# Reordering the steps of a fused attention and int8 layer, with two PSUM banks for the first projections

## What is computed

```python
q = (x @ Wq + bq).reshape(b, t, H, D)
k = (x @ Wk + bk).reshape(b, t, HKV, D)
v = (x @ Wv + bv).reshape(b, t, HKV, D)
q = q * cos + rotate_half(q) * sin
k = k * cos + rotate_half(k) * sin
attn = jnp.einsum('bikgd,bjkd->bkgij', qg, k) * scale      # causal mask, softmax
out = jnp.einsum('bkgij,bjkd->bikgd', p, v).reshape(b, t, H * D)
x = _layernorm(x + out @ Wo)
q, in_scale = per_token_quant_int8(x)                        # round(x / scale), scale = absmax / 127
acc = jnp.einsum('bsk,nk->bsn', q, weight)
x = _layernorm(x + (acc * in_scale * w_scale + bias).astype(float16))
```

## Time and profile before

| what | value |
|---|---|
| median of three runs | 174.61 us (174.49 to 174.62) |
| the profiled execution, its own time | 174.22 us |
| its span, first to last instruction | 172.3 us |
| instructions in it | 4469 |
| share of the span busy: TensorE, VectorE, ScalarE, GpSimd | 85%, 82%, 71%, 50% |
| mean granted clock of TensorE | 0.957 |

### The profile page before, as it was taken

How to read it: one execution, slowest core, us unless ns; L and a number is a source line. 1 busy time by engine, 2 the same in 40 slices (tenths; PEclk the granted TensorE clock), 3 DMA queues, 4 the chain that set the end, 5 groups by cost and what they waited for, 6 DMA issues and landing times. The chain is left out here.

```text
span 172.3 us, 4469 instructions
## 1 busy us (share of the span) xinstructions
PE 147.3 (85%) x1552; PEld 87.3 (51%) x1552; DVE 140.8 (82%) x345; ACT 123.0 (71%) x231; POOL 85.7 (50%) x191
## 2 busy tenths in 40 slices
PE   1768999999999999999999989999999988893330
PEld 0154464565665556656676456655666554551100
DVE  3408789898899599899899789989999997787582
ACT  3244577887797879898988776989878898993000
POOL 1051794224078868213899996032488504465111
PEclk9999999999999999999999999999999999997555
DMA  5986000000000001000000101000001200001101
GB/s 138 259 142 186 2 5 0 4 4 0 10 4 0 6 0 65 1 6 1 2 8 0 56 12 59 8 0 8 0 2 47 80 4 2 2 4 61 61 0 61
DMA packets 5463, 5.63 MB, mean 33 GB/s; under 512 B 1217, under 2 KB 4674, under 8 KB 5442
## 3 DMA queue, kind: packets, MB, share of 16 engines
q1 hardware_dynamic: 5298, 5.16, 10.9%
q10 hardware_dynamic: 144, 0.20, 0.4%
HBM read 3.12 MB, written 2.10 MB: 30 GB/s over the span
## 5 line engine op out<-in xcount | busy, mean ns | idle before, releaser
L415 ACT ACTIVATE prob<-score_ps 128x512 bf16<-128x512 f32 x160 | 89.6, 600 | 16.8 <-PE score_ps L616 8.2
L507 DVE TENSOR_REDUCE nmax<-front_ps 128x1 f32<-128x320 f32 (+21 forms) x137 | 87.6, 680 | 13.2 <-PE front_ps L660 12.3
L612 PE MATMUL score_ps<-qkA 128*128 128x512 bf16 x160 | 57.9, 379 | 0.9 <-ACT prob L415 0.5
L658 PE MATMUL front_ps<-qkA 128*128 128x384 bf16 (+9 forms) x176 | 50.6, 334 | 1.7 <-DVE nmax L507 1.4
L627 PEld LDWEIGHTS mix_ps<-qkv,prob 128*128 128x128 bf16 x640 | 26.1, 96 | 14.3 <-ACT prob L415 3.5
L660 PE MATMUL front_ps<-tab 128*128 128x32 bf16 (+2 forms) x176 | 32.3, 187 | 0.0
L627 PE MATMUL mix_ps<-qkv,prob 128*128 128x17 bf16 x640 | 30.2, 171 | 1.3 <-ACT prob L415 1.2
L658 PEld LDWEIGHTS front_ps<-qkA 128*128 128x128 bf16 x176 | 17.2, 98 | 16.6 <-issue 6.8
L616 PE MATMUL score_ps<-tab 128*128 128x512 bf16 x64 | 24.2, 378 | 0.0
L424 ACT ACTIVATE qkA<-side_ps 128x1024 bf16<-128x1024 bf16 x16 | 16.4, 1024 | 5.5 <-PE side_ps L649 5.3
L354 POOL TENSOR_TENSOR rot<-qkv,tab 128x320 bf16<-128x320 bf16 x14 | 10.4, 745 | 18.6 <-ACT qkv L420 18.6
(11 more groups left out here) (61 smaller groups left out, 175.6 us busy)
## 6 DMA issues: line engine op xcount, KB each, us to landing
out<-fo SPq DMA_DIRECT2D x7, 256.0 KB, 2.2
xt<-in_xT SPq DMA_DIRECT2D x1, 768.0 KB, 6.3
qkA<-peakT SPq DMA_DIRECT2D x32, 4.0 KB
xt<-in_xT SPq DMA_DIRECT2D x2, 128.0 KB, 3.0
bfc<-in_bias SPq DMA_DIRECT2D x2, 128.0 KB, 7.4
out<-fo SPq DMA_DIRECT2D x2, 128.0 KB, 1.7
tab<-in_table SPq DMA_DIRECT2D x1, 232.0 KB, 3.1
wqkv<-in_wqkv_in ACTq DMA_DIRECT2D x1, 192.0 KB
```

The lines of the kernel that those rows point to most:

```text
L415: act.activation(prob[:, u % PROB_RING, :].rearrange("p (h t c) -> p t h c", h=GH, c=SUB), score_ps[u % SCORE_RING][:, :].rearrange("p (t ...
L507: dve.tensor_reduce(to, src, AX.X, ALU.max, negate=True).then_inc(max_ok, 1)
L612: mm = pe.matmul(score_ps[u % SCORE_RING][:, :].rearrange("p (t c) -> p t c", c=TOK), qkA[:, n, GH + g, TOK * j:TOK * (j + 1)], qkA[:, n, ...
L658: pe.matmul(bank, qkA[:, n, t, TOK * i:TOK * (i + 1)], qkA[:, n, GH + g:GH + g + fit, 0:wide], start=True, stop=False)
```

## The change

Three things. First, TensorE runs 26 matmuls of a one-row constant with itself into `mix_ps` before it waits for the weights. Nothing reads the result. Second, the projections P1, P2 and P3 (`HEAD_TILES`) write `dense_ps` instead of `side_ps`; their copies and ropes wait for that bank's semaphores. Third, all five lists of `ORDER` have another order, with the same steps in each. Other additions are switched off or have no user: `LINEAR_ACT` is False and `NORM_FAST` is 0, the steps n, d and l on ScalarE, r on VectorE and N on GpSimd stand in no list, and `rden` has two slots instead of one.

```diff
+LINEAR_ACT = False
+HEAD_TILES = (1, 2, 3, )
+WARM = 26
+NORM_FAST = 0
...
     "tensor": """
-        P0 P1 P2 T0 T1 F0 F1 F2 F3 F4 T2 F5 F6 G0 F7 F8 F9 P3 F10 F11 F12 P4 S0 S1 F13 F14 F15 P5 S2 F16 F17 T3 F18 S3 F19 F20
+        P0 P1 P2 T0 P3 F0 T1 F1 F2 F3 F4 F5 T2 F6 F7 F8 F9 P4 F10 F11 G0 F12 P5 F13 F14 F15 T3 F16 F17 S0 F18 G1 S1 F19 F20 W0
...
     "gpsimd": """
-        R2 w0 K0 R3 K1 R4 R5 K2 R6 R7 K3 K4 K5 m0 R8 Q0 R9 K6 R10 H0 z0 Y0 R11 K7 m1 K8 Q1 K9 m2 R12 Q2 R13 H1 H2 K10 z1 Y1 z2
-        R14 Y2 R15 m3 K11 K12 Q3 K13 m4 Q4 H3 K14 H4 z3 Y3 z4 Y4 m5 K15 Q5 m6 H5 z5 Y5 m7 z6 m8 z7 z8
+        R2 R3 K0 w0 R4 K1 R5 K2 R6 R7 K3 m0 R8 K4 Q0 R9 K5 H0 z0 K6 R10 Y0 R11 m1 K7 K8 Q1 R12 m2 K9 R13 H1 Q2 z1 K10 Y1 H2 z2
+        R14 m3 Y2 K11 R15 K12 Q3 m4 K13 Q4 H3 H4 z3 Y3 K14 z4 Y4 m5 K15 Q5 m6 H5 m7 z5 Y5 m8 z6 z7 z8
...
-SIDE_USES = [step for step in steps("tensor") if step[0] in "PTG"]
-DENSE_USES = [step for step in steps("tensor") if step[0] in "UMDL"]
+def in_dense(step):
+
+    return step[0] in "UMDL" or step[0] == "P" and step[1] in HEAD_TILES
+
+
+SIDE_USES = [step for step in steps("tensor") if step[0] in "PTG" and not in_dense(step)]
+DENSE_USES = [step for step in steps("tensor") if in_dense(step)]
...
+        def project_bank(u):
+
+            if u in HEAD_TILES:
+                return dense_ps, dense_full, dense_free, dense_at("P", u)
+            return side_ps, side_full, side_free, side_at("P", u)
...
                 elif kind == "p":
-                    act.wait_ge(side_full, side_at("P", u) + 1)
-                    act.activation(qkv[:, u, :, 0:VAT + DH], side_ps[:, 0:PC].rearrange("p (g c) -> p g c", g=GROUPS),
-                                   ACT.Copy).then_inc(side_free, 1)
+                    bank, filled, freed, uses = project_bank(u)
+                    act.wait_ge(filled, uses + 1)
+                    act.activation(qkv[:, u, :, 0:VAT + DH], bank[:, 0:PC].rearrange("p (g c) -> p g c", g=GROUPS),
+                                   ACT.Copy).then_inc(freed, 1)
...
             pe.wait_ge(ones_set, 1)
+            for _ in range(WARM):
+                pe.matmul(mix_ps[:, 0:128], ones[:, :], ones[:, :], start=True, stop=True)
             pe.wait_ge(weights_in, 16 * 2)
```

More of the change, by code:

```diff
@@ L121 @@
-        N13 X135 X136 B5 s6 q5 a6 B6 d5 q6 l5 N14 d6 l6 Z5 H6 s7 Z6 a7 B7 N15 Y6 q7 s8 a8 B8 d7 q8 l7 H7 d8 Z7 l8 H8 Y7 Z8 Y8
+        R0 R1 X0 X1 X2 X3 X4 X5 X6 X7 X8 X9 X10 X11 X12 X13 X14 X15 X16 X17 X18 X19 X20 N0 X21 X22 X23 X24 X25 X26 X27 X28 X29
+        N1 X30 X31 X32 X33 X34 s0 X35 X36 X37 X38 X39 B0 X40 X41 N2 X42 X43 q0 X44 X45 X46 d0 X47 X48 l0 X49 X50 X51 X52 X53
+        Z0 X54 X55 X56 X57 N3 X58 X59 X60 N4 X61 X62 X63 X64 s1 X65 X66 X67 X68 X69 N5 X70 X71 X72 X73 B1 X74 X75 s2 X76 X77
@@ L226, in build @@
         qsc = sb("qsc", [128, ALL], bf16)
+        qscf = sb("qscf", [128, ALL], fp32)
+        mixs = sb("mixs", [128, 2, HEADS * VA], fp32)
         qrec = sb("qrec", [128, ALL], fp32)
@@ L441, in _ @@
                         one.then_inc(dense_free if m == ms[-1] else x1_ok, 1)
+                elif kind == "n":
+                    act.wait_ge(weighed, LAST_SCORE[u] + 1)
+                    need(act, att_ok, u - 1)
+                    act.activation(mixs[:, u % 2, :], mix_ps[:, 0:HEADS * VA], ACT.Copy).then_inc(mixed_ok, 1)
+                elif kind == "d":
+                    ms, part, done = tiles_of(u)
+                    act.wait_ge(dense_full, dense_at("D", u) + 1)
+                    act.activation(q8T[:, KC * ms[0]:KC * done, :],
+                                   dense_half[:, 0:KC * TOK * len(ms)].rearrange("p (a c) -> p a c", c=TOK),
+                                   ACT.Copy).then_inc(dense_free, 1)
+                elif kind == "l":
+                    ms, part, done = tiles_of(u)
+                    act.wait_ge(dense_full, dense_at("L", u) + 1)
+                    for m in ms:
+                        one = act.activation(fo[:, m, :], dense_ps[:, (m - ms[0]) * HID:(m - ms[0] + 1) * HID], ACT.Copy,
+                                             scale=qscf[:, m:m + 1])
+                        one.then_inc(dense_free if m == ms[-1] else fo_ok, 1)
                 elif kind == "Y":
@@ L541, in _ @@
                     dve.wait_ge(qsc_ok, done)
+                    if LINEAR_ACT and u not in FAST:
+                        dve.tensor_copy(qscf[:, part], qsc[:, part])
                     dve.reciprocal(qrec[:, part], qsc[:, part]).then_inc(qrec_ok, len(ms))
@@ L623, in _ @@
                     if u == FIRST_SCORE[tile]:
-                        need(pe, att_ok, tile)
+                        if tile <= NORM_FAST:
+                            need(pe, mixed_ok, tile)
+                        else:
+                            need(pe, att_ok, tile)
                     pr = prob[:, u % PROB_RING, :].rearrange("p (h c) -> p h c", h=GH)
@@ L632, in _ @@
                         pe.wait_ge(xt_in[(0, 2, TILES).index(u)], 16)
-                    pe.matmul(side_ps[:, 0:PC], ones[:, :], bqkv[:, :], start=True, stop=False)
+                    bank, filled, _, _ = project_bank(u)
+                    pe.matmul(bank[:, 0:PC], ones[:, :], bqkv[:, :], start=True, stop=False)
                     for c in range(KC):
-                        mm = pe.matmul(side_ps[:, 0:PC], xt[:, c, TOK * u:TOK * (u + 1)], wqkv[:, c, :],
+                        mm = pe.matmul(bank[:, 0:PC], xt[:, c, TOK * u:TOK * (u + 1)], wqkv[:, c, :],
                                        start=False, stop=c == KC - 1)
-                    mm.then_inc(side_full, 1)
+                    mm.then_inc(filled, 1)
                 elif kind == "T":
```

104 lines of the change are left out of this document (60 added, 44 removed).

## The result

The changed kernel takes **166.75 us** (median of 4 runs, 166.25 to 166.84) against 174.62 us for the kernel before beside it (4 runs, 174.49 to 174.66): a ratio of 0.9545, 95% interval 0.9525 to 0.9564. That is 7.9 us faster. The prediction said 171.5 us and 169.0 to 174.0; the direction was right, the time lies outside the range.

What follows compares the result with a forecast made beforehand. VectorE was taken to bound the middle, ScalarE's exps close behind, with serial chains at both ends. Start -3.1, middle +0.5 and end -0.5 sum to -3.1 us: 174.61 to 171.5 us, range 169.0 to 174.0.

Steps and rivals of the forecast that it cites:

- The middle is therefore VectorE's: Middle: VectorE, busy 116.28 of 130 us, sets the pace, with ScalarE's exps close behind at 109.24.
- the term of +0.5 us: Middle: VectorE waits 0 to 1.6 us at an earlier normalization; 0.5 us was taken as the loss.
- Rival 2: Middle: the exps become the bound, ScalarE keeps its old idle time; 173.1 us, chance 0.13.
- The start, -3.1: Start: a shorter projection ladder and faster clock bring the first reduce to 9.5 instead of 12.59 us.
- I take full speed from P2 on: Start: gapless TensorE work brings full clock from the third projection; 0.9 us of the first reduce's gain.
- rival 1: Start: the constant matmuls don't lift the clock, first reduce at 10.4 us; 172.4 us in all, chance 0.14.
- No hole opens: Start: the second transposes follow the first maxima matmul, while the first four reduces occupy VectorE until 11.5 us.
- The end, -0.5: End: net of a normalization's gain of 1.2 us and a cost of 0.7 us, bounds -1.7 and +0.9.
- N15: End: the last normalization follows its matmuls without VectorE being late, -1.2 us.
- Y6: End: this 0.73 us step, before in a hole, now stands between B8 and q8 in the chain, +0.7 us.
- N2: Middle: normalization moved ahead by seven reduces, reached at 42.9 us, waits 0 to 1.6 us for the 24th exp.
- rival 3: Middle: VectorE blocks at earlier normalizations, 0.86 us each; slower, 177.0 us with seven, chance 0.10.

Runs made afterwards that it cites:

- e1: Changed kernel with its new orders, but all projections in the side bank and no constant matmuls: 169.36 us, ratio 0.9709.
- e7: Kernel before, with every reduce reading only the first half of its columns: 172.38 us, ratio 0.9869.
- e8: Kernel before, without the 64 causal mask matmuls of the score steps: 171.49 us, ratio 0.9847.
- e4: Changed kernel with the old orders up to the last reduce and the new ones from there on: 172.61 us, ratio 0.989.
- e17: Changed kernel with only value steps W0 to W111 moved, as far behind their scores as in the old order: 178.96 us, ratio 1.0264.

## Why the prediction was wrong

**"The middle is therefore VectorE's" is the step that failed,** and with it the term of +0.5 us, which measured -4.3. The working took VectorE's busy 116.28 of 130 us as the pace and left TensorE out because its busy rows overlap. It then priced the reorder of the middle only at the waits it might add, and gave nothing for gaps it might close. But each engine had gaps: from X4 to X136 VectorE is busy for 113.8 of 126.0 us, ScalarE 103.7, TensorE by start distances 109.9. The step order was what changed, and with the same work TensorE's idle time fell from 15.5 to 11.2 us. "The same steps run on each engine, so busy time stays" was true and said nothing on the gaps. The half reduces show it: 31 us less work on the supposed bound gave 2.2 us of time, and 1.2 in the new order.

**The exps' pace** was the number at which it could have been seen. I gave the first 24 exps their old idle time of 4.2 us "again", from a start at 18.6. They started at 20.04, not earlier but 0.5 us later than before, and were through at 43.0: 23.0 us where the old order took 25.3. ScalarE's idle time changed with the order. Rival 2 took it as kept, too, and fell with it.

**What in the order does it** I can narrow but not settle. Shown: the gain of the middle needs neither bank nor constants (e1); 3.5 of the 4.3 us arise between X32 and X96; TensorE's idle time falls from 15.5 to 11.2 us, most of it at F steps; and it does not survive a piecewise transfer (a cut at X96, the transposes' place, four placings of W and N). Transposes T12 and T13 back at their old place cost 2.8 us in the new order, by the wait of P14 for the shared bank, but their new place in the old order gains nothing. That the gain is the fit of all five lists is an inference from these misses and not shown; which set of moves would be enough wasn't found, and the cause of the middle's gain stays open to that extent.

**The start, -3.1, measured -2.1 at X0 and -1.7 at X4.** The ladder's steps were right: P2 starts at 6.81 (forecast 6.65), T0 behind it, P3 next. The size failed at "I take full speed from P2 on": X0 came at 10.46, rival 1's 10.4. The gapless work before P2 (1.03 to 6.2 us) was in fact longer than that before T2 in the kernel before (11.30 to 13.9), and no full clock came with it. Nor is the rise a fixed answer to a start: with the same work as before T2, TensorE was still slow at 14.8 us in e7 and e8. "No hole opens" was also wrong, by X1's 0.88 us: T1 at half speed takes 1.06. T2 came at 12.93, not 11.2; VectorE had reduces without a hole from 11.64 to 15.07, so that cost nothing. w0 kept its place in time (14.18), so the moves on GpSimd cost nothing visible, as assumed.

The Trainium skill, page TensorE: Matmul & The Clock Gate, Part 1: The HAM clock gate, calls the slow ramp worth under 1% of a typical kernel's span. The prediction's estimate from it, which the sum did not use, was 1.7 us at most for the constants. Their net effect stayed inside that: no constants, 26 of one row, 26 of 128 rows and 52 of 128 rows gave 166.30, 166.75, 166.51 and 166.23 us, all within 0.5 us. The ramp itself costs more here than the page says, 2.6 us from P0's start to X4 (9.39 against 6.82 us, one trace each), 1.6% of the span of 165.0. The half microsecond from run to run that the prediction took from the same part is too little as well: with the start of the changed kernel the rise came at 11.3 to 13.1 us. The measurements decide.

**The end, -0.5, measured -1.4.** N15 was right: -1.2 forecast, -1.4 measured from X136 on, of which 0.9 is N15's nearness to its matmuls (0.4 us behind them, not 1.3); e4 shows that this gain belongs to the end's own order. D6, moved ahead of S158, did no harm. The term that was mis-sized is Y6: +0.7 forecast, +0.1 measured. Y6 does stand between B8 and q8 (155.82), but the chain behind it became shorter by as much: d7 stands at 151.06 (at 163.28 before), so L7's result is there when l7 comes up at 156.91, right behind q8. I had named that ("D7 and d7 leave the chain") without giving it a price.

**N2 and rival 3.** N2 was forecast at 42.9 with a wait of 0 to 1.6 us; it came at 44.18 without one. The 1.3 us are the start's missing ones. The wait of rival 3 can be made, as e17 shows with 11.1 us of it, but in the changed kernel VectorE's reciprocals do not wait.

**The best version** of these runs is the changed kernel without constants, or with 52 of them: 166.30 and 166.23 us against 166.75. The ranges overlap, and 0.5 us is what can be said at most.

## What to carry to other kernels

Where several engines are each 80 to 90% busy and run fixed lists that wait for each other, the busiest need not be the bound. Then a reorder must be judged by the gaps that it closes, on TensorE by the distance between matmul starts, and not by busy time alone. Test such a claim by taking work from the supposed bound before trusting it: here 27% less work on VectorE gave 1.3% of the time. And a handwritten order is best taken over whole: single features of a better one cost 1 to 28 us in the other here.
